# Layer 1 attention: probability blocks transposed by DVE and transfers, value products across the slot boundary, and four scalings for keys and queries

## The chip, the cores and the metric

The kernel runs on one core of one Trainium2 chip. The metric is the device time of one execution in microseconds, the median of several executions. The engines are TensorE (PE in the profile), VectorE (DVE), ScalarE (ACT), GpSimd (POOL) and SyncE (SP, which here only issues DMA transfers).

## The reference

Two transformer layers on 1024 tokens of width 512, in float32: layer 0 (linear attention with 32 heads, then experts), layer 1 (softmax attention with 32 heads of width 128, then a gated MLP with dequantised weights), each part followed by a residual and a layer norm. The change is in layer 1's attention:

```python
q = rmsnorm(hidden_states @ Wq + bq, gq)      # per head of 128
k = rmsnorm(hidden_states @ Wk + bk, gk)
v = hidden_states @ Wv + bv
scores = einsum('bnhd,bmhd->bhnm', q, k) / sqrt(128)
attn = softmax(scores, axis=-1)
out = einsum('bhnm,bmhd->bnhd', attn, v) @ Wo + bo
```

## The kernel before, in words

Every float32 matmul is made of three float32r matmuls (`three_pass`, lines 82 to 84): each operand is split into a high part (an ACT copy) and a low part (a subtraction on DVE or POOL), and high x high, high x low and low x high are added up in PSUM. So each tile that TensorE reads needs two more operations first.

`l1_attention` runs over 32 heads. Tokens are in 8 tiles of 128 (`NT`), and two tiles make a batch (`BATCH` = 2, four batches a head). Each engine has its own instruction queue, written out in order by a function `step` that is called once a head; it goes through 8 slots s = 0 to 7, and an engine that reaches a wait on a semaphore holds up everything behind it in its queue. Slots are software-pipelined: in slot s of head h an engine does

- the projection of one token tile of the next head (`project_tile` on TensorE, 12 matmuls of 384 columns; `take` on DVE adds the bias, L1434),
- in even slots the squares (`square`, ACT L1272), their sums and means (`means`, DVE L1441 and L1444), the inverse root on POOL (`inverse_rms`, L1236) and the scaling of the keys by it (`scale_k`, DVE L1449); in odd slots the transposes of keys and queries (`transpose_kq`, L1357), their high parts on ACT (L1279, L1280) and low parts on DVE (L1456, L1457); the query's own factor is put into the exponential,
- the scores of one query tile against all 1024 keys (`scores`, 6 matmuls of 512 columns into the banks `s_ps`), their row maximum and the shift made from it (`maxima`, DVE L1464 and L1466), and the exponential (`exponent`, ACT L1304, which writes `prob`),
- for the query tile of the slot before: 8 transposes of 128x128 on TensorE into `t_ps` (`transpose_probs`, L1390), the high part `pT_hi` (ACT L1298) and the low part `pT_lo` (DVE L1472),
- half of the value products of a finished batch (`values`, 12 matmuls of 256 columns into `o_ps`); behind the second half the parts of the output (ACT L1291, DVE L1484), and `output_tile` (3 matmuls of 512 columns) with the addition on DVE (L1493).

The heads 2 to 29 are a loop of two heads, the others are written out; the last head has no next head to project. The weights of a head come in one load (`AttentionWeights.load`) and are split in three pieces (L1039 on ACT, L1046 on POOL), the output weights in one (L1329, L1256). SP's queue issues three loads a head.

Layer 0 transposes its keys in another way (`move_k`, L352): DVE transposes blocks of 32x32 in place of the whole (L665), and 16 transfers move the 32-row groups to where they belong.

## Time and profile before

| what | value |
|---|---|
| median of 3 runs | 3258.07 us (3256.71 to 3260.59) |
| the profiled execution | 3259.28 us, its span 3257.5 us |
| busy share of the span: PE, DVE, ACT, POOL | 97%, 63%, 43%, 30% |
| mean granted TensorE clock | 0.991 of full speed |
| layer 1 attention | from about 1240 us to 2986 us |

The span is the time from the first to the last instruction. Busy time doesn't count waiting. A timeline row is one instruction (or a run of like ones, "x4"): start, length, engine, line, operation, tile written and tiles read; in brackets the idle time ahead of it and who ended it.

### The profile page before, as it was taken

How to read it: one execution, taken by the hardware profiler on the slowest of the kernel's cores; microseconds unless marked ns; L12 is line 12 of the kernel's file. 1: busy time of each engine (PE TensorE's matmuls, PEld its weight loads, DVE VectorE, ACT ScalarE, POOL GpSimd, SP SyncE). 2: the span in 40 equal slices, each digit the busy share in tenths (PEclk: the TensorE clock that was granted, in tenths of full speed). 3: DMA queues.
4: the chain of work that ended last, by engine and by line, in shares of the span. 5: the costliest groups of instructions: out<-in, count | busy, mean ns of one | idle time of the engine just before them, and what ended most of it. 6: DMA issues, size and time to landing. Idle time of an engine off the chain costs nothing. (4 is left out here: it accounts for less than half of the span.)

```text
span 3257.5 us, 58748 instructions
## 1 busy us (share of the span) xinstructions
PE 3165.4 (97%) x19680; PEld 2888.2 (89%) x19680; DVE 2067.9 (63%) x3445; ACT 1388.4 (43%) x2375; POOL 972.3 (30%) x819
## 2 busy tenths in 40 slices
PE   7999999999999978999999999999999999997998
PEld 7989989989989857999999999999999999996786
DVE  3445444455454457777777777777777777776555
ACT  3333333333333323555555555555555555554221
POOL 3333333333333322222222222222222222211765
PEclk9999999999999989999999999999999999999999
DMA  4122122122122101000000000000000000002541
GB/s 128 50 61 60 48 61 60 48 61 60 48 61 60 35 23 34 32 16 31 15 31 15 31 15 31 16 30 24 22 30 16 31 15 31 15 7 79 160 140 55
DMA packets 127177, 145.32 MB, mean 45 GB/s; under 512 B 15488, under 2 KB 91280, under 8 KB 126992
## 3 DMA queue, kind: packets, MB, share of 16 engines
q1 hardware_dynamic: 126272, 143.77, 14.7%
q8 instruction: 35, 0.57, 0.1%
q10 hardware_dynamic: 816, 0.79, 0.1%
q14 instruction: 22, 0.18, 0.0%
q0 software_dynamic: 32, 0.02, 0.0%
HBM read 125.63 MB, written 2.10 MB: 39 GB/s over the span
## 5 line engine op out<-in xcount | busy, mean ns | idle before, releaser
L1304 ACT ACTIVATE b_prob<-b_s_ps,b_shift,b_rstd 128x1024 f32<-128x1024 f32 x252 | 304.2, 1207 | 580.9 <-DVE b_shift L1466 580.9
L1464 DVE TENSOR_REDUCE b_row_max<-b_s_ps 128x1 f32<-128x1024 f32 x252 | 307.2, 1219 | 78.5 <-PE b_s_ps L84 78.4
L82 PE MATMUL b_pj_kq<-b_w_hi,xT_hi 128*128 128x384 f32 x1008 | 341.5, 339 | 1.2 <-DVE b_nat L1434 1.2
L84 PE MATMUL b_pj_kq<-b_w_hi,xT_lo 128*128 128x384 f32 x1008 | 341.9, 339 | 0.0
L83 PE MATMUL b_pj_kq<-b_w_lo,xT_hi 128*128 128x384 f32 x1008 | 341.5, 339 | 0.0
L506 ACT ACTIVATE a_sig<-a_pj 128x512 f32<-128x512 f32 x192 | 114.8, 598 | 486.7 <-PE a_pj L84 486.7
L82 PE MATMUL a_pj<-b_w_hi,xT_hi 128*128 128x256 f32 x1024 | 295.5, 289 | 11.7 <-DVE xT_lo L647 11.1
L84 PE MATMUL a_pj<-b_w_hi,xT_lo 128*128 128x256 f32 x1024 | 289.9, 283 | 0.0
L83 PE MATMUL a_pj<-b_w_lo,xT_hi 128*128 128x256 f32 x1024 | 289.4, 283 | 0.0
L1236 POOL TENSOR_TENSOR b_rstd<-b_mean_sq,power 128x4 f32<-128x4 f32 x128 | 128.9, 1007 | 527.7 <-DVE b_mean_sq L1444 524.4
L1390 PE MATMUL b_t_ps<-ident,b_prob 128*128 128x128 f32 x2048 | 265.6, 273 | 4.8 <-ACT b_prob L1304 4.4
L1046 POOL TENSOR_TENSOR b_w_lo<-b_w_raw,b_w_hi 128x512 fp32r<-128x512 f32 x96 | 123.2, 1285 | 486.3 <-ACT b_w_hi L1039 455.6
L706 DVE TENSOR_TENSOR a_kv_nat<-a_pj,a_sig 128x512 f32<-128x512 f32 x128 | 88.5, 692 | 273.0 <-ACT a_sig L506 271.8
L711 DVE TENSOR_TENSOR a_acc<-a_acc,a_y_ps 128x512 f32<-128x512 f32 x252 | 170.4, 676 | 136.1 <-PE a_y_ps L84 136.1
L1390 PEld LDWEIGHTS b_t_ps<-ident,b_prob 128*128 128x128 f32 x2048 | 230.5, 141 | 6.8 <-ACT b_prob L1304 6.8
L401 POOL TENSOR_TENSOR b_w_lo<-b_w_raw,b_w_hi 128x512 fp32r<-128x512 f32 x96 | 124.5, 1297 | 331.5 <-ACT b_w_hi L457 324.6
L82 PE MATMUL b_s_ps<-b_k_hi,b_q_hi 128*128 128x512 f32 x504 | 219.1, 435 | 0.0
L82 PEld LDWEIGHTS a_pj<-b_w_hi,xT_hi 128*128 128x128 f32 x1024 | 194.5, 190 | 14.6 <-issue 11.9
L1456 DVE TENSOR_TENSOR b_k_lo<-b_pj_kq,b_k_hi 128x256 fp32r<-128x256 f32 x128 | 54.3, 425 | 230.2 <-ACT b_q_hi L1280 230.2
L82 PEld LDWEIGHTS b_pj_kq<-b_w_hi,xT_hi 128*128 128x128 f32 x1008 | 189.1, 188 | 12.6 <-issue 1.7
L83 PEld LDWEIGHTS b_pj_kq<-b_w_lo,xT_hi 128*128 128x128 f32 x1008 | 189.2, 188 | 11.4
L84 PE MATMUL b_s_ps<-b_k_hi,b_q_lo 128*128 128x512 f32 x504 | 198.8, 394 | 0.0
(272 smaller groups left out, 9107.6 us busy)
## 6 DMA issues: line engine op xcount, KB each, us to landing
b_w_raw<-in_w SPq DMA_DIRECT2D x32, 768.0 KB, 4.3
b_w_raw<-in_w SPq DMA_DIRECT2D x95, 256.0 KB, 3.2
a_k_raw<-a_k_blocks SPq DMA_DIRECT2D x512, 32.0 KB, 1.8
a_w_raw<-in_w SPq DMA_DIRECT2D x32, 256.0 KB, 2.7
a_ow_raw<-in_ow SPq DMA_DIRECT2D x32, 256.0 KB, 3.1
...
```

The source lines that it names most:

```text
L82: pe.matmul(out, w_hi, x_hi, start=first, stop=False)
L83: pe.matmul(out, w_hi, x_lo, start=False, stop=False)
L84: return pe.matmul(out, w_lo, x_hi, start=False, stop=last)
L401: pool.tensor_tensor(w_lo[t][:, :, :], w_raw[t][:, :, :], f(w_hi[t][:, :, :]), ALU.subtract).then_inc(w_lo_done, 1)
L506: act.activation(out, pj[half][:, :], ACT.Sigmoid).then_inc(sig, 1)
L706: dve.tensor_tensor(out, pj[half][:, :], sig_tmp[half][:, :], ALU.mult).then_inc(silu, 1)
L711: dve.tensor_tensor(acc[:, t, :], acc[:, t, :], y_bank(h, t)[:, :], ALU.add).then_inc(y_added, 1)
L1046: pool.tensor_tensor(self.lo[b][:, :, cut], self.raw[:, :, cut], f(self.hi[b][:, :, cut]), ALU.subtract).then_inc(self.lo_done, 1)
L1236: pool.tensor_tensor(rstd[bg][:, BATCH * i:BATCH * (i + 1), :].rearrange("p t k -> p (t k)"), mean_sq[:, :, :].rearrange("p t k -> p (t k) ...
L1304: act.activation(prob[:, :], score_banks(h, t)[:, :], ACT.Exp, bias=shift[:, t:t + 1], scale=rstd[b][:, t, 1:2], accum_out=row_sum[:, t:t ...
L1390: last = pe.transpose(t_ps[:, cut], prob[:, cut], sh.ident[:, :])
L1464: dve.tensor_reduce(row_max[:, t:t + 1], score_banks(h, t)[:, :], AX_X, ALU.max).then_inc(max_done, 1)
```

## The change

The probabilities are no longer transposed by TensorE. DVE transposes 32x32 blocks of `prob` into `blocks` (`transpose_blocks`), for two query tiles; SP then issues 16 transfers (`move`) that carry 32-row groups into `pT_lo`, as raw values. ACT copies them to `pT_hi` in two halves of a batch (`prob_hi`), and POOL makes the low part in place (`prob_lo`), which was DVE's work. The value products and outputs of a batch come two slots later than before; the first half of a batch's value products stands at the end of an odd slot, the second half at the start of the even slot that follows. `s_ps` has two banks (the transposes' bank is free), `prob` two buffers. The row maximum is written negated as the shift. Keys and queries are both scaled by their inverse root, with four operations by a per-partition scalar for a batch (`scale_kq`), and the exponential has no scale. The weight splits stand in slots 1, 2 and 4 in place of 0, 2 and 4.

```diff
+        BLK = 32
+        GROUPS = P // BLK
+        MOVED = 16 * GROUPS * GROUPS
...
-        prob = sb("prob", [P, TOK])
-        row_max = sb("row_max", [P, NT])
+        prob = [sb(f"prob{i}", [P, TOK]) for i in range(2)]
+        blocks = [sb(f"blocks{i}", [P, GROUPS, NT, BATCH, BLK]) for i in range(2)]
...
-        pT_hi = [mlp.pT0[0], sb("pT_hi1", [P, NT, WIDE], F32R)]
-        pT_lo = [mlp.pT0[1], sb("pT_lo1", [P, NT, WIDE], F32R)]
+        pT_hi = [mlp.pT0[0], sb("pT_hi1", [P, GROUPS, NT, BATCH * BLK], F32R)]
+        pT_lo = [mlp.pT0[1], sb("pT_lo1", [P, GROUPS, NT, BATCH * BLK], F32R)]
...
-        s_ps = bank("s_ps", [P, TOK])
-        t_ps = bank("t_ps", [P, TOK])
+        s_ps = [bank(f"s_ps{i}", [P, TOK]) for i in range(2)]
...
-            n = (s - 3) % 8
-            if s >= 3:
+            n = (s - 5) % 8
+            if s >= 5:
...
+        def split_part(h, cur, rest, s):
+
+            n = (s - 4) % 8
+            if s >= 4:
+                return (h, n // 2, n % 2) if cur else None
+            return (h - 1, n // 2, n % 2) if rest else None
...
-            if s >= 5:
-                return (h, b, s - 5) if cur else None
-            return (h - 1, 1 - b, s + 3) if rest else None
+            if s >= 7:
+                return (h, b, s - 7) if cur else None
+            return (h - 1, 1 - b, s + 1) if rest else None
...
+        SPLITS = {1: 0, 2: 1, 4: 2}
...
+            def move(h, i):
+
+                sp.wait_ge(blocked, NT * h + BATCH * (i + 1))
+                to = f(pT_lo[i % 2][:, :, :, :])
+                for a in range(GROUPS):
+                    for g in range(GROUPS):
+                        sp.dma_start(to[a * BLK:(a + 1) * BLK, g].rearrange("p m n -> p (m n)"),
+                                     blocks[i % 2][g * BLK:(g + 1) * BLK, a].rearrange("p m u q -> p (m u q)")).then_inc(
+                            moved[i % 2], 16)
...
+            def step(h, b, cur, rest, nxt, more):
+                if cur and more:
+                    aw.load(sp, w, h + 2)
+                    load_bias(h + 2, b)
+                if rest:
+                    move(h - 1, NB - 1)
+                if cur:
+                    move(h, 0)
+                if nxt:
+                    load_output_weights(h + 1)
+                if cur:
+                    move(h, 1)
+                    move(h, 2)
...
+            def prob_lo(h, i, part):
+
+                pool.wait_ge(pT_hi_done, 2 * NB * h + 2 * i + part + 1)
+                cut = slice(part * NT // 2, (part + 1) * NT // 2)
+                pool.tensor_tensor(pT_lo[i % 2][:, :, cut, :], f(pT_lo[i % 2][:, :, cut, :]), f(pT_hi[i % 2][:, :, cut, :]),
+                                   ALU.subtract).then_inc(pT_lo_done, 1)
...
+            def prob_hi(h, i, part):
+
+                act.wait_ge(moved[i % 2], MOVED * (2 * h + i // 2 + 1))
                 wait(act, pv, NB * h + i - 1)
...
+                cut = slice(part * NT // 2, (part + 1) * NT // 2)
+                act.activation(pT_hi[i % 2][:, :, cut, :], f(pT_lo[i % 2][:, :, cut, :]), ACT.Copy).then_inc(pT_hi_done, 1)
 
             def exponent(h, b, t):
                 act.wait_ge(shift_done, NT * h + t + 1)
-                wait(act, p_tr, NT * h + t)
-                act.activation(prob[:, :], score_banks(h, t)[:, :], ACT.Exp, bias=shift[:, t:t + 1],
-                               scale=rstd[b][:, t, 1:2], accum_out=row_sum[:, t:t + 1]).then_inc(exp_done, 1)
+                wait(act, blocked, NT * h + t - 1)
+                act.activation(prob[t % 2][:, :], s_ps[t % 2][:, :], ACT.Exp, bias=shift[:, t:t + 1],
+                               accum_out=row_sum[:, t:t + 1]).then_inc(exp_done, 1)
...
+                pe.wait_ge(pT_lo_done, 2 * NB * h + 2 * i + part + 1)
                 if part == 0:
-                    pe.wait_ge(pT_lo_done, NT * h + BATCH * (i + 1))
...
+                    if s % 2 == 0 and quarter(h, b, cur, rest, s):
+                        values(*quarter(h, b, cur, rest, s))
...
-                    if quarter(h, b, cur, rest, s):
-                        values(*quarter(h, b, cur, rest, s))
                     if nxt and s % 2:
                         transpose_kq(h + 1, s // 2)
-                    if rest and s == 0:
-                        transpose_probs(h - 1, NT - 1)
-                    if cur and s:
-                        transpose_probs(h, s - 1)
...
+                    if s % 2 and quarter(h, b, cur, rest, s):
+                        values(*quarter(h, b, cur, rest, s))
...
-            def scale_k(g, bg, i):
+            def scale_kq(g, bg, i):
                 dve.wait_ge(rstd_ready, NB * g + i + 1)
-                dve.tensor_tensor(nat[i][:, :, 0:HD], nat[i][:, :, 0:HD],
-                                  rstd[bg][:, BATCH * i:BATCH * (i + 1), 0:1].broadcast_to([P, BATCH, HD]),
-                                  ALU.mult).then_inc(k_scaled, 1)
+                for u in range(BATCH):
+                    for k in range(2):
+                        part = nat[i][:, u, k * HD:(k + 1) * HD]
+                        last = dve.tensor_scalar(part, part, rstd[bg][:, BATCH * i + u, k:k + 1], None, ALU.mult)
+                last.then_inc(kq_scaled, 1)
...
-                dve.tensor_reduce(row_max[:, t:t + 1], score_banks(h, t)[:, :], AX_X, ALU.max).then_inc(max_done, 1)
-                dve.wait_ge(max_done, NT * h + t + 1)
-                dve.tensor_scalar(shift[:, t:t + 1], row_max[:, t:t + 1], rstd[b][:, t, 1:2], -1.0,
-                                  ALU.mult, ALU.mult).then_inc(shift_done, 1)
-
-            def prob_lo(h, t):
-                i, at = t // BATCH, (t % BATCH) * P
-                dve.wait_ge(pT_hi_done, NT * h + t + 1)
-                dve.tensor_tensor(pT_lo[i % 2][:, :, at:at + P], t_ps[:, :].rearrange("p (m n) -> p m n", m=NT),
-                                  f(pT_hi[i % 2][:, :, at:at + P]), ALU.subtract).then_inc(pT_lo_done, 1)
+                dve.tensor_reduce(shift[:, t:t + 1], s_ps[t % 2][:, :], AX_X, ALU.max, negate=True).then_inc(shift_done, 1)
...
+            def transpose_blocks(h, t):
+
+                i, u = t // BATCH, t % BATCH
+                dve.wait_ge(exp_done, NT * h + t + 1)
+                if u == 0:
+                    wait(dve, moved[i % 2], MOVED * (2 * h + i // 2))
+                dve.transpose(blocks[i % 2][:, :, :, u, :].rearrange("p a m q -> p m a q"),
+                              prob[t % 2][:, :].rearrange("p (m a q) -> p m a q", a=GROUPS, q=BLK)).then_inc(blocked, 1)
...
-                        prob_lo(h - 1, NT - 1)
+                        transpose_blocks(h - 1, NT - 1)
                     if cur and s:
-                        prob_lo(h, s - 1)
-                    if not early:
-                        for t in scored_in(h, cur, s):
-                            maxima(h, b, t)
+                        transpose_blocks(h, s - 1)
+                    for t in scored_in(h, cur, s):
```

DVE, an even slot in the loop (names as in the text above: `b_nat` are the projections, `b_o_lo` the output's low part). Before:

```order
L1441 TENSOR_REDUCE b_sq_sum<-b_sq 128x4
L1444 TENSOR_SCALAR b_mean_sq<-b_sq_sum 128x4
...
L1434 TENSOR_TENSOR b_nat<-b_pj_kq,b_bias 128x384
L1449 TENSOR_TENSOR b_nat<-b_nat,b_rstd 128x2x128
L1484 TENSOR_TENSOR b_o_lo<-b_o_ps,b_o_hi 128x256
L1472 TENSOR_TENSOR pT_lo<-b_t_ps,pT_hi 128x8x128
L1464 TENSOR_REDUCE b_row_max<-b_s_ps 128x1
L1466 TENSOR_SCALAR b_shift<-b_row_max,b_rstd 128x1
L1493 SCALAR_TENSOR_TENSOR x_nat<-b_y_ps,b_row_inv,x_nat 128x512
```

and with the change:

```order
L1468 TENSOR_REDUCE b_sq_sum<-b_sq 128x4
L1471 TENSOR_SCALAR b_mean_sq<-b_sq_sum 128x4
...
L1461 TENSOR_TENSOR b_nat<-b_pj_kq,b_bias 128x384
L1479 TENSOR_SCALAR b_nat<-b_nat,b_rstd 128x128 x4
L1513 TENSOR_TENSOR b_o_lo<-b_o_ps,b_o_hi 128x4x2x32
L1501 STREAM_TRANSPOSE b_blocks<-b_prob 128x8x4x32
L1493 TENSOR_REDUCE b_shift<-b_s_ps 128x1
L1522 SCALAR_TENSOR_TENSOR x_nat<-b_y_ps,b_row_inv,x_nat 128x512
```

The subtraction L1472 and the shift L1466 are gone, the block transpose L1501 stands ahead of the maximum L1493 in every slot, and the one scaling L1449 is four (L1479).

TensorE, an even slot, each block by its first rows (`b_pj_kq` is the projection, `b_o_ps` the value products, `b_s_ps` the scores, `b_y_ps` the output). Before:

```order
L82 MATMUL b_pj_kq<-b_w_hi,xT_hi 128x384
...
L84 MATMUL b_pj_kq<-b_w_hi,xT_lo 128x384
...
L82 MATMUL b_o_ps<-pT_hi,b_v_hi 128x256
...
L84 MATMUL b_o_ps<-pT_hi,b_v_lo 128x256
...
L1390 MATMUL b_t_ps<-ident,b_prob 128x128 x8
L82 MATMUL b_s_ps<-b_k_hi,b_q_hi 128x512
...
L82 MATMUL b_y_ps<-b_ow_hi,b_o_hi 128x512
```

and with the change:

```order
L82 MATMUL b_o_ps<-b_pT_hi,b_v_hi 128x256
...
L84 MATMUL b_o_ps<-b_pT_hi,b_v_lo 128x256
L82 MATMUL b_pj_kq<-b_w_hi,xT_hi 128x384
...
L84 MATMUL b_pj_kq<-b_w_hi,xT_lo 128x384
...
L82 MATMUL b_s_ps<-b_k_hi,b_q_hi 128x512
...
L82 MATMUL b_y_ps<-b_ow_hi,b_o_hi 128x512
```

The transposes L1390 are gone, and the value products stand ahead of the projection.

POOL, from an even slot to the next but one (`b_rstd` is the inverse root, `b_v_lo` the low part of the values, `b_w_lo` that of the weights). Before:

```order
L1236 TENSOR_TENSOR b_rstd<-b_mean_sq,power 128x4
L1243 TENSOR_TENSOR b_v_lo<-b_nat,b_v_hi 128x256
...
L1236 TENSOR_TENSOR b_rstd<-b_mean_sq,power 128x4
...
L1046 TENSOR_TENSOR b_w_lo<-b_w_raw,b_w_hi 128x4x128
L1243 TENSOR_TENSOR b_v_lo<-b_nat,b_v_hi 128x256
```

and with the change:

```order
L1267 TENSOR_TENSOR b_rstd<-b_mean_sq,power 128x4
...
L1281 TENSOR_TENSOR b_pT_lo<-b_pT_lo,b_pT_hi 128x4x256
L1274 TENSOR_TENSOR b_v_lo<-b_nat,b_v_hi 128x256
...
L1281 TENSOR_TENSOR b_pT_lo<-b_pT_lo,b_pT_hi 128x4x256
...
L1267 TENSOR_TENSOR b_rstd<-b_mean_sq,power 128x4
```

Behind each inverse root there is now a subtraction of 128x1024 for the probabilities (L1281), and another in the odd slot behind the values' low part.

## Rows read from the trace of the kernel before

**Rows 1.** Busy time by stretch (us, instructions), clock, DMA; layer 1 attention.
```profile
1600.00:2000.00 400.00, 400.00 (x2565) 377.01 (x2565) 297.16 (x506) 212.08 (x359) 89.62 (x90) 1.00 0.07 22
```

**Rows 2.** Timeline of ACT: start us, length us, line, operation, tiles.
```profile
1913.07 0.38 ACT L1279 ACTIVATE b_k_hi<-b_pj_kq 128x256 fp32r<-128x256 f32 x1 [0.75 <-PE b_pj_kq L1357]
1913.35 0.47 ACT L1280 ACTIVATE b_q_hi<-b_pj_kq,b_gain 128x256 fp32r<-128x256 f32 x1
1913.94 1.03 ACT L1298 ACTIVATE b_pT_hi<-b_t_ps 128x1024 fp32r<-128x1024 f32 x1
...
1924.20 1.21 ACT L1304 ACTIVATE b_prob<-b_s_ps,b_shift,b_rstd 128x1024 f32<-128x1024 f32 x1 [2.67 <-DVE b_shift L1466]
...
1925.40 0.62 ACT L1039 ACTIVATE b_w_hi<-b_w_raw 128x512 fp32r<-128x512 f32 x1
...
1977.84 1.21 ACT L1304 ACTIVATE b_prob<-b_s_ps,b_shift,b_rstd 128x1024 f32<-128x1024 f32 x1 [2.67 <-DVE b_shift L1466]
```

**Rows 3.** Timeline of TensorE (PE), first matmul of each block.
```profile
1986.51 1.04 PE L1390 MATMUL b_t_ps<-ident,b_prob 128*128 128x128 f32 x8
1987.30 0.47 PE L82 MATMUL b_s_ps<-b_k_hi,b_q_hi 128*128 128x512 f32 x1
...
1989.46 0.33 PE L82 MATMUL b_pj_kq<-b_w_hi,xT_hi 128*128 128x384 f32 x1
...
1991.57 0.28 PE L82 MATMUL b_o_ps<-pT_hi,b_v_hi 128*128 128x256 f32 x1
...
1992.99 0.60 PE L1357 MATMUL b_pj_kq<-ident,b_nat 128*128 128x128 f32 x4
```

**Rows 4.** Timeline of DVE, layer 0.
```profile
619.99 1.23 DVE L665 STREAM_TRANSPOSE a_k_blocks<-a_kv_nat 128x1024 f32<-128x1024 f32 x1
```

**Rows 5.** Timeline of DVE, layer 1.
```profile
1959.67 0.17 DVE L1444 TENSOR_SCALAR b_mean_sq<-b_sq_sum 128x4 f32<-128x4 f32 x1
...
1961.31 0.42 DVE L1484 TENSOR_TENSOR b_o_lo<-b_o_ps,b_o_hi 128x256 fp32r<-128x256 f32 x1
...
1962.93 1.21 DVE L1464 TENSOR_REDUCE b_row_max<-b_s_ps 128x1 f32<-128x1024 f32 x1
...
1964.96 0.55 DVE L1434 TENSOR_TENSOR b_nat<-b_pj_kq,b_bias 128x384 f32<-128x384 f32 x1
1965.43 0.15 DVE L1480 RECIPROCAL b_row_inv<-b_row_sum 128x2 f32<-128x2 f32 x1
```

**Rows 6.** Timelines of DVE and POOL at the layer norms and the first head.
```profile
1237.81 1.91 DVE L169 TENSOR_SCALAR x_nat<-x_nat,ln_mv,ln_rstd 128x512 f32<-128x512 f32 x4
...
1256.74 1.48 DVE L1449 TENSOR_TENSOR b_nat<-b_nat,b_rstd 128x256 f32<-128x256 f32 x1
...
1256.67 1.26 POOL L1046 TENSOR_TENSOR b_w_lo<-b_w_raw,b_w_hi 128x512 fp32r<-128x512 f32 x1
...
2999.68 0.89 DVE L169 TENSOR_SCALAR x_nat<-x_nat,ln_mv,ln_rstd 128x512 f32<-128x512 f32 x1
```

**Rows 7.** Groups of POOL instructions, 1500 to 2700 us: busy us, mean ns.
```profile
L1046 POOL TENSOR_TENSOR b_w_lo<-b_w_raw,b_w_hi 128x512 fp32r<-128x512 f32 x67 | 85.7, 1280 | 358.6 <-ACT b_w_hi L1039 358.6
L1243 POOL TENSOR_TENSOR b_v_lo<-b_nat,b_v_hi 128x256 fp32r<-128x256 f32 x89 | 66.2, 743 | 113.9 <-ACT b_v_hi L1285 113.9
```

**Rows 8.** Timelines of SP and ACT, layer 0: sixteen transfers and their reader.
```profile
32.07 10.12 SPq L352 DMA_DIRECT2D a_k_raw<-a_k_blocks  x16
...
43.45 0.63 ACT L474 ACTIVATE a_k_T<-a_k_raw 128x512 f32<-128x512 f32 x1 [5.83 <-DMA a_k_raw<-a_k_blocks]
```

**Rows 9.** Timeline of TensorE: a value product after a wait.
```profile
2951.74 0.39 PE L82 MATMUL b_o_ps<-pT_hi,b_v_hi 128*128 128x256 f32 x1 [0.30 <-DVE pT_lo L1472]
```

**Rows 10.** Timelines of ACT and DVE, the last head.
```profile
2942.54 1.21 ACT L1304 ACTIVATE b_prob<-b_s_ps,b_shift,b_rstd 128x1024 f32<-128x1024 f32 x1 [2.67 <-DVE b_shift L1466]
...
2973.91 1.20 ACT L1304 ACTIVATE b_prob<-b_pj_kq,b_shift,b_rstd 128x1024 f32<-128x1024 f32 x1
...
2985.47 0.75 DVE L1493 SCALAR_TENSOR_TENSOR x_nat<-b_pj_kq,b_row_inv,x_nat 128x512 f32<-128x512 f32 x1
```

More of the change, by code:

```diff
@@ L1117, in l1_attention @@
         y_ps = bank("y_ps", [P, HALF])
-        ln_banks = [s_ps[:, 0:HALF], s_ps[:, HALF:], t_ps[:, 0:HALF], t_ps[:, HALF:]]
+        ln_banks = [s[:, j * HALF:(j + 1) * HALF] for s in s_ps for j in range(2)]
         w_lo_done, proj = aw.lo_done, aw.proj
@@ L1257, in step @@
                                            ALU.subtract).then_inc(ow_lo_done, 1)
-                    if nxt and more and s in (0, 2, 4):
-                        aw.split_low(pool, h + 2, b, s // 2)
+                    if nxt and more and s in SPLITS:
+                        aw.split_low(pool, h + 2, b, SPLITS[s])
             steps(pool, step)
@@ L1375, in scores @@
                     pe.wait_ge(kq_lo_done, NB * (h + 1))
-                wait(pe, exp_done, NT * h + (t - 1 if peeled(h, HEADS - 1) and t else t))
+                wait(pe, exp_done, NT * h + t - 1)
                 cut = slice(t * P, (t + 1) * P)
@@ L1380, in scores @@
                     keys = slice(j * HALF, (j + 1) * HALF)
-                    last = three_pass(pe, score_banks(h, t)[:, keys], q_hi[b][:, cut], q_lo[b][:, cut],
+                    last = three_pass(pe, s_ps[t % 2][:, keys], q_hi[b][:, cut], q_lo[b][:, cut],
                                       k_hi[b][:, keys], k_lo[b][:, keys], True, True)
                 last.then_inc(scored, 1)
-            def transpose_probs(h, t):
-                pe.wait_ge(exp_done, NT * h + t + 1)
-                wait(pe, pT_lo_done, NT * h + t)
-                for m in range(NT):
-                    cut = slice(m * P, (m + 1) * P)
-                    last = pe.transpose(t_ps[:, cut], prob[:, cut], sh.ident[:, :])
-                last.then_inc(p_tr, 1)
             def output_tile(h, b, t):
```

66 lines of the change are left out of this document (27 added, 39 removed).

## The prediction

> **What bounds the kernel now.** I read the table of busy time by stretch first. In a stretch of 400 us inside layer 1's attention TensorE is busy for 400.00 us at full clock, DVE for 297, ACT for 212, POOL for 90 [rows 1]. So this stage goes by the sum of its matmuls, and the view of waits agrees: it names no wait of TensorE there, only of the other engines. Then the timelines. The reader should see that DVE and ACT hand work to each other in every slot, and that this has cover only because a slot is long. On ACT the same slot's exponentials lie 53.64 us apart from one head to the next (1924.20 to 1977.84) [rows 2]: four pairs of an even and an odd slot, 13.41 us a pair.
>
> **What is removed.** TensorE loses eight transposes a slot: they start at 1986.51 and the scores at 1987.30, 0.79 us [rows 3], 6.3 us a head. If TensorE stayed the bound, a head would take 47.4 us. The question is whether the rest of the loop can run in 11.8 us a pair.
>
> **What is added, by engine.** DVE: the subtraction of 128x1024 leaves and a block transpose of the same size comes, 1.23 us in layer 0 [rows 4]; the shift leaves; one scaling a pair becomes four of 128x128. A DVE operation that waits for nothing starts 0.08 us before the end of the one ahead (0.55 long, the next after 0.47) [rows 5]. Four scalings of 128x512 by per-partition scalars take 1.91 us, so 0.46 apart [rows 6]; one operation of 128x4 lasts 0.17 [rows 5], so 0.09 apart. By columns 128x128 comes to 0.18; I take 0.20, 0.80 for four, bounds 0.36 and 1.84. POOL: two subtractions of 128x1024 a pair. The rows give 0.743 for 256 columns and 1.280 for 512 [rows 7], 2.1 ns a column, so 2.37; upper bound twice 1.28, 2.56. SP: 16 transfers a pair, each of 32 rows of 2 KB. Layer 0 issues such 16 with rows of 1 KB in 10.12 us from 32.07 on, and ACT reads them at 43.45, 11.38 us after the first issue [rows 8]. That is 10.1 of 13.4 us a pair, and three loads a head beside it, so SP isn't the bound if an issue doesn't grow with its row. ACT's amount of work stays.
>
> **The chain that I expect to set the pace.** It is closed through all four engines, from the row maximum of an even slot to that of the next even slot. A hand-over costs some 0.05. (1) Maximum 1.21 + 0.05 [rows 5]. (2) Exponential, 1.20 to ACT's next start (1924.20 to 1925.40) [rows 2]. (3) In the odd slot the copies of values, keys and queries, all ahead of the probability copy in ACT's queue: 0.28 for the keys, the same for the values, 0.37 for the queries (ACT starts 0.10 before the end of the one ahead), 0.93 [rows 2]. (4) Probability copy, second half: 1.03 + 0.05 [rows 2]. (5) POOL's subtraction of that half: 2.37 + 0.05. (6) TensorE: the second half of the value products stands first in the even slot and waits for it: 12 matmuls, 1.42 [rows 3], and 0.11 for the start after a wait (0.39 beside 0.28) [rows 3, 9]. (7) Behind it the projection, 2.11 [rows 3], and an estimated 0.20 until its last result can be read. (8) DVE takes the projection, 0.47 [rows 5]. (9) Four scalings, 0.80. (10) Low part of the output, 0.34 [rows 5]. (11) Block transpose, 1.15, then the maximum. Sum: 1.26 + 1.20 + 0.93 + 1.08 + 2.42 + 1.53 + 2.31 + 0.47 + 0.80 + 0.34 + 1.15 = 13.49 us a pair. In slots 2 and 4 a weight copy stands between (2) and (3), 0.62 long, 0.52 to the next [rows 2]. A head: 4 x 13.49 + 1.04 = 55.0 us, 1.3 above the 53.7 of now. So what TensorE saves turns into waiting, some 8 us a head, ahead of the second value half.
>
> Before the change no such chain passed through TensorE and POOL together: POOL did nothing for the probabilities, and the value products came behind the projection.
>
> **Edges.** 29 heads of this kind: +38. Head 0 has no values before slot 5 and head 30 projects nothing in slots 6 and 7. Both are some 2 us shorter than the others now, since TensorE has less to do in them, and less of the new chain falls away there than of TensorE's sum; I add an estimated 2 and 3. Head 31 has no projections, and its seven steps from exponential to exponential take 31.4 us (2942.54 to 2973.91) [rows 10]. After, a batch's transfers are in a chain of two pairs: 11.5 + 1.08 + 4.79 (two halves on POOL) + 1.7 + 0.8 + 1.23 = 21.1, 10.5 a pair, 36.6 for seven steps: +5. The drain, from the last exponential to the end of the last addition (2985.47 + 0.75), is 12.3 us [rows 10]. After: exponential 1.2, transpose 1.28, transfers 11.5, 1.08, 4.79, values 1.7, output copies 0.9, two outputs 1.6, addition 0.75 = 24.8: +12.5. Together 38 + 5 + 5 + 12.5 = 61. The profiled execution took 3259.28 us with a span of 3257.5, 1.2 above the median of 3258.07, so the same difference holds for both: 3258 + 61 = **3319 us**, 1.9% slower.
>
> **What is hidden, and by what.** Transfers: a batch is blocked 0.08 us after the maximum of an even slot starts and has landed 11.5 later. The odd slot's maximum comes 5.4 after the even one (1.26 + 1.20, copies 0.56, low keys and queries an estimated 1.24, transpose 1.15), so counted from it the batch lands at 6.2. Its first copy on ACT ends at 7.2; behind it waits the exponential of the even slot, due only at 5.8 + 0.80 + 0.34 + 1.15 + 1.26 = 9.3. So the transfers have two us of cover, and each further one goes into the chain. The second bank of the scores and the factor that leaves the exponential (now applied in the scaling of queries) cost nothing: no score waits.
>
> **A rule against this change.** The row first: before the loop the scaling of the keys (two SBUF inputs) took 1.48 us at 1256.74, while POOL subtracted from 1256.67 on for 1.26, where 256 columns take 0.42 elsewhere [rows 5, 6]; and a 128x512 scaling by per-partition scalars took 0.89 at 2999.68, where four take 1.91 otherwise [rows 6], with a subtraction on POOL in both cases. In the loop the scalings come right behind POOL's inverse root, and POOL's next work is a first-half subtraction. By my times the scalings run from 5.8 (1.45 for POOL's half, + 1.53 + 2.31 + 0.47) to 6.6 us after the odd maximum, and the subtraction starts at 7.2, after slots with a weight copy at 6.7. They miss each other, by 0.6 us in two pairs of a head and 0.1 in the other two; at these times the rows add nothing.
> The Trainium skill, SBUF — State Buffer, section "Who interferes with whom", says that a `tensor_scalar` in a two-port mode and a GpSimd operation exclude each other, and that the one that came first holds the ports to its end. The trace agrees with it (1.48 for 0.42). By it the sum would be 2.4 higher in every pair in which POOL comes first.
>
> **Rivals.**
> A, POOL and the scalings meet (slower still). If transfers land 0.3 us earlier or the scalings take 0.3 longer, then in two pairs a head the last scaling waits for POOL's 2.37: +4.7 a head, 29 x 4.7 = 136, 3455 us; in all four pairs, from some 0.8 on, 3530 or more. Against: a row of 2 KB lands later than one of 1 KB, if anything.
> B, transfers are the bound: if an issue goes with its bytes, 16 x 1.27 = 20 us a pair, a head 83, some 4100 us. Against: from the end of the last issue to the reader's start there are 1.3 us (43.45 - 42.19) [rows 8], so the bytes of a transfer don't hold the queue for long.
> C, the other sign: POOL's half is ready earlier than I have it, and the chain doesn't pass through TensorE. Then a pair goes by DVE and ACT alone, over squares, means and POOL's root, which I estimate to be ready at 5.1 where the take ends at 5.8: 12.8 us; with scalings at 0.36, 12.4, and four weight copies of 0.52: a head 51.7, 29 x -2.0 - 5 + 17 = -46, 3212 us. It decides at a pair of 13.0 us: below that the kernel is faster. With TensorE the bound after all it would be 3258 - 29 x 6.3 - 10 + 17 = 3082. For it: DVE would be busy for some 40 of 47 us only. Against: nearly each term of the 13.49 is a row.
> D, nothing measurable: the chain is 0.5 shorter, and heads gain what the edges lose.
>
> **How the numbers follow.** Forecast 0.45, its own range from the scalings (0.36; or 1.2) and POOL's 2.56, 116 pairs: -51 and +70, so 3268 to 3390. A 0.25, B 0.05, C 0.14, D 0.05; others of the same sign as the forecast (a slower copy out of SBUF, a clock that falls in the gap of the drain) 0.06. The range 3240 to 3470 leaves out B, most of C and the worst of A. Faster by over 0.2% 0.14, within 0.2% (about what three runs can tell here) 0.05, slower 0.81.
>
> **What would show it.** In the loop TensorE busy for some 47 of 55 us, waiting at the first value matmul of even slots for POOL's low parts; DVE's take waiting for the projection; POOL's subtractions 2.4 us long; SP issuing 64 transfers in 40 of 55 us; scalings of 0.28 us. Wrong if scalings last 1 us and more (A), if ACT's copies wait for transfers and exponentials behind them (B), if TensorE is busy throughout or the scalings wait for the root alone (C).

## The result

The changed kernel takes 3526.8 us (median of four executions, 3484.56 to 3529.72) where the kernel before takes 3257.8 (3256.71 to 3260.59): 1.080 times, 95% interval 1.073 to 1.087. The profiled execution is the fastest of the four, 3484.56 us with a span of 3482.8, and what is read below is its trace. The forecast was 3319 us, slower, with a range up to 3470: the direction was right, the size was not.

Busy time by stretch after the change (columns as in [rows 1]): TensorE (first busy column) 336 us of 400 instead of 400, POOL (last) 201 instead of 90, and the granted clock, 1.00 before, is 0.95.

```profile
1600.00:2000.00 400.00, 336.19 (x1847) 305.59 (x1846) 273.81 (x476) 176.35 (x314) 201.14 (x130) 0.95 0.36 90
```

The page's groups of the new operations, for [rows 2, 5 and 7]: busy us, mean ns, idle before. Each operation has nearly the length that was forecast for it. What stands out is the idle time.

```profile
L1343 ACT ACTIVATE b_prob<-b_s_ps,b_shift 128x1024 f32<-128x1024 f32 x256 | 285.5, 1115 | 722.0 <-DVE b_shift L1493 722.0
L1281 POOL TENSOR_TENSOR b_pT_lo<-b_pT_lo,b_pT_hi 128x1024 fp32r<-128x1024 f32 x128 | 303.5, 2371 | 166.8 <-ACT b_pT_hi L1338 166.8
L1501 DVE STREAM_TRANSPOSE b_blocks<-b_prob 128x1024 f32<-128x1024 f32 x256 | 316.1, 1235 | 4.5 <-ACT b_prob L1343 4.5
L1493 DVE TENSOR_REDUCE b_shift<-b_s_ps 128x1 f32<-128x1024 f32 x256 | 303.7, 1186 | 2.0 <-PE b_s_ps L84 2.0
L1461 DVE TENSOR_TENSOR b_nat<-b_pj_kq,b_bias 128x384 f32<-128x384 f32 x252 | 139.1, 552 | 241.7 <-PE b_pj_kq L84 241.6
```

From one head's first exponential to the next the trace shows 53.7, 55.1, 55.3, 58.2 us, and from the ninth such step on 61.4 or 61.5 (but for the last two). The forecast had 55.0 for all. So a head as forecast exists, at the start of the stage, and then something is added. It is added by the pair: of the 119 pairs of slots in heads 1 to 30, 69 take 13.4 to 14.1 us from odd maximum to odd maximum and 50 take 16.6 to 17.3. The slow ones are always the same two of a head, the pair around slot 4 and the pair around slot 6. Here is one pair of each kind. First DVE in the quick one: maximum at 2041.09, take of the projection at 2046.44 (5.35 later; forecast 5.3), four scalings 0.86 long, next odd maximum at 2054.55, 13.46 later (forecast 13.49).

```profile
2041.09 1.18 DVE L1493 TENSOR_REDUCE b_shift<-b_s_ps 128x1 f32<-128x1024 f32 x1
...
2046.44 0.56 DVE L1461 TENSOR_TENSOR b_nat<-b_pj_kq,b_bias 128x384 f32<-128x384 f32 x1 [1.48 <-PE b_pj_kq L84]
2046.91 0.86 DVE L1479 TENSOR_SCALAR b_nat<-b_nat,b_rstd 128x128 f32<-128x128 f32 x4
...
2054.55 1.19 DVE L1493 TENSOR_REDUCE b_shift<-b_s_ps 128x1 f32<-128x1024 f32 x1
```

POOL's first-half subtraction in that pair starts 0.71 us after the scalings have ended (the forecast said 0.6):

```profile
2048.48 2.40 POOL L1281 TENSOR_TENSOR pT_lo<-pT_lo,pT_hi 128x1024 fp32r<-128x1024 f32 x1 [2.44 <-ACT pT_hi L1338]
```

Then the slow one, DVE and POOL. The take is 7.11 us after the maximum, the four scalings last 2.46 us, and they lie inside POOL's subtraction (2014.18 to 2016.58). The next odd maximum is 17.26 later.

```profile
2007.21 1.19 DVE L1493 TENSOR_REDUCE b_shift<-b_s_ps 128x1 f32<-128x1024 f32 x1
...
2014.32 0.56 DVE L1461 TENSOR_TENSOR b_nat<-b_pj_kq,b_bias 128x384 f32<-128x384 f32 x1 [2.72 <-PE b_pj_kq L84]
2014.79 2.46 DVE L1479 TENSOR_SCALAR b_nat<-b_nat,b_rstd 128x128 f32<-128x128 f32 x4
2017.17 0.41 DVE L1513 TENSOR_TENSOR b_o_lo<-b_o_ps,b_o_hi 128x256 fp32r<-128x256 f32 x1
...
2022.58 0.42 DVE L1485 TENSOR_TENSOR b_k_lo<-b_pj_kq,b_k_hi 128x256 fp32r<-128x256 f32 x1 [1.54 <-ACT b_q_hi L1320]
...
2024.47 1.19 DVE L1493 TENSOR_REDUCE b_shift<-b_s_ps 128x1 f32<-128x1024 f32 x1
2014.18 2.40 POOL L1281 TENSOR_TENSOR pT_lo<-pT_lo,pT_hi 128x1024 fp32r<-128x1024 f32 x1 [1.49 <-ACT pT_hi L1338]
```

Why is the take late? TensorE in the two pairs, first matmul of the value half, of the projection, and of the scores behind it. In the slow pair:

```profile
2008.78 0.39 PE L82 MATMUL b_o_ps<-b_pT_hi,b_v_hi 128*128 128x256 f32 x1 [2.16 <-POOL b_pT_lo L1281]
...
2010.46 0.52 PE L82 MATMUL b_pj_kq<-b_w_hi,xT_hi 128*128 128x384 f32 x1
...
2013.96 0.39 PE L82 MATMUL b_s_ps<-b_k_hi,b_q_hi 128*128 128x512 f32 x1
```

and in the quick one:

```profile
2042.58 0.39 PE L82 MATMUL b_o_ps<-b_pT_hi,b_v_hi 128*128 128x256 f32 x1 [2.45 <-POOL b_pT_lo L1281]
...
2044.12 0.34 PE L82 MATMUL b_pj_kq<-b_w_hi,xT_hi 128*128 128x384 f32 x1
...
2046.24 0.39 PE L82 MATMUL b_s_ps<-b_k_hi,b_q_hi 128*128 128x512 f32 x1
```

Both begin 1.5 to 1.6 us after the maximum, behind a wait of 2.2 and 2.45 us. But the projection takes 3.50 us in one and 2.12 in the other. The same stretches by the microsecond (the third number from the end is the granted clock) show what differs: the clock is at its half level, 1.2 instead of 2.4 GHz.

```profile
2009.00:2010.00 1.00, 1.00 (x10) 1.00 (x10) 0.05 (x1) 1.00 (x3) 0.00 (x0) 1.00 0.55 131
2010.00:2011.00 1.00, 1.00 (x6) 1.00 (x6) 0.29 (x1) 0.90 (x3) 0.71 (x1) 0.56 0.37 88
2011.00:2012.00 1.00, 1.00 (x4) 1.00 (x4) 0.56 (x2) 0.16 (x1) 0.89 (x2) 0.50 0.46 109
2012.00:2013.00 1.00, 1.00 (x4) 1.00 (x4) 0.00 (x0) 0.00 (x0) 0.69 (x1) 0.50 0.49 94
2013.00:2014.00 1.00, 1.00 (x6) 1.00 (x6) 0.00 (x0) 0.96 (x1) 0.00 (x0) 0.74 0.70 223
2014.00:2015.00 1.00, 1.00 (x6) 0.83 (x5) 0.68 (x2) 0.10 (x1) 0.82 (x1) 1.00 0.03 10
```

So this slow pair takes 3.80 us more than the quick one. 1.38 of it is the projection and 0.38 the value half, the start and the take's own wait at the lower clock (scalings 7.58 instead of 5.82 us after the maximum); 1.60 is the length of the scalings; the last 0.44 is not new, it is a weight copy on ACT that this pair has and the other hasn't (DVE's wait for the queries' copy 1.54 instead of 1.10), and was in the forecast. Compared with a quick pair of the same place in the head, a slow one costs 3.2 us around slot 4 (17.25 beside 14.0) and 3.1 around slot 6 (16.63 beside 13.55): the scalings start 1.6 later and last 1.5 to 1.8 longer. Over heads 1 to 30 the granted clock stands at half in 51 spells, 178 us in all, and in none in the kernel before; each of the 50 slow pairs has one, and no quick pair has. The slow pairs come to 157 us (23 x 3.2 + 27 x 3.1). Added to the forecast that gives 3476, and with the 8 us by which the drain was too short (below) 3484, beside 3484.56 measured; the closeness is partly luck, since the quick heads (55.1 to 55.3) and the edges were a little off too. This is a reading of one trace; it doesn't show which of the two causes the other, nor whether either would cost anything alone. The theory (M): the clock falls after TensorE's wait for POOL, that makes the take late, and the late scalings meet POOL. The rivals: POOL and the scalings meet whatever the clock (L); the clock has no part in it (N); the landing of the transfers sets the pace and the rest only fills it (T); the form of the four scalings is dear by itself (F).

### The profile page after: what moved, and what is told of

Read it like the earlier page. It is cut to its first block and busy times, and to the rows that moved or that the text cites. A ratio compares the mean times of both kernels' runs of the same rounds, so it can differ in the third digit from the quotient of the medians.

```text
span 3482.8 us, 57425 instructions
## 1 busy us (share of the span) xinstructions
PE 3079.6 (88%) x17632; PEld 2755.3 (79%) x17632; DVE 2113.5 (61%) x3573; ACT 1344.6 (39%) x2375; POOL 1578.8 (45%) x1075
## 5 line engine op out<-in xcount | busy, mean ns | idle before, releaser
L1343 ACT ACTIVATE b_prob<-b_s_ps,b_shift 128x1024 f32<-128x1024 f32 x256 | 285.5, 1115 | 722.0 <-DVE b_shift L1493 722.0
L82 PE MATMUL b_pj_kq<-b_w_hi,xT_hi 128*128 128x384 f32 x1008 | 376.3, 373 | 7.7 <-DVE b_nat L1461 7.7
L1281 POOL TENSOR_TENSOR b_pT_lo<-b_pT_lo,b_pT_hi 128x1024 fp32r<-128x1024 f32 x128 | 303.5, 2371 | 166.8 <-ACT b_pT_hi L1338 166.8
L1281 POOL TENSOR_TENSOR pT_lo<-pT_lo,pT_hi 128x1024 fp32r<-128x1024 f32 x128 | 304.1, 2376 | 165.0 <-ACT pT_hi L1338 165.0
L1501 DVE STREAM_TRANSPOSE b_blocks<-b_prob 128x1024 f32<-128x1024 f32 x256 | 316.1, 1235 | 4.5 <-ACT b_prob L1343 4.5
L1493 DVE TENSOR_REDUCE b_shift<-b_s_ps 128x1 f32<-128x1024 f32 x256 | 303.7, 1186 | 2.0 <-PE b_s_ps L84 2.0
L1461 DVE TENSOR_TENSOR b_nat<-b_pj_kq,b_bias 128x384 f32<-128x384 f32 x252 | 139.1, 552 | 241.7 <-PE b_pj_kq L84 241.6
L82 PE MATMUL b_o_ps<-b_pT_hi,b_v_hi 128*128 128x256 f32 x512 | 154.2, 301 | 143.8 <-POOL b_pT_lo L1281 143.8
L82 PE MATMUL b_o_ps<-pT_hi,b_v_hi 128*128 128x256 f32 x512 | 152.3, 297 | 134.8 <-POOL pT_lo L1281 134.8
L82 PEld LDWEIGHTS b_o_ps<-b_pT_hi,b_v_hi 128*128 128x128 f32 x512 | 99.7, 195 | 160.5 <-POOL b_pT_lo L1281 157.7
```

The costliest lines, as they stand in the source:

```text
L82: pe.matmul(out, w_hi, x_hi, start=first, stop=False)
L1281: pool.tensor_tensor(pT_lo[i % 2][:, :, cut, :], f(pT_lo[i % 2][:, :, cut, :]), f(pT_hi[i % 2][:, :, cut, :]), ALU.subtract).then_inc(pT_l ...
L1343: act.activation(prob[t % 2][:, :], s_ps[t % 2][:, :], ACT.Exp, bias=shift[:, t:t + 1], accum_out=row_sum[:, t:t + 1]).then_inc(exp_done, 1)
L1461: dve.tensor_tensor(nat[i][:, u, :], project_bank(g, t), bias_sb[bg][:, :], ALU.add).then_inc(taken, 1)
L1493: dve.tensor_reduce(shift[:, t:t + 1], s_ps[t % 2][:, :], AX_X, ALU.max, negate=True).then_inc(shift_done, 1)
L1501: dve.transpose(blocks[i % 2][:, :, :, u, :].rearrange("p a m q -> p m a q"), prob[t % 2][:, :].rearrange("p (m a q) -> p m a q", a=GROUPS ...
```

## The experiments

**TensorE kept busy in its wait.** This tells the clock from the rest: nothing is taken away, work is added.

```
 if s % 2 == 0 and quarter(h, b, cur, rest, s):
+    (heads 1 to 30) wait(pe, kq_lo_done, NB * (h + 1) + s // 2)
+    for _ in range(20): pe.transpose(kq_ps[:, 0, 0:P], sh.ident[:, :], sh.ident[:, :])
     values(*quarter(h, b, cur, rest, s))
```

> Edit: TensorE gets 20 more 128x128 transposes of the identity (0.10 us each, 2.0 us) in every even slot of heads 1 to 30, ahead of its wait for POOL's low parts, into a bank that nobody reads then; their results are not used. It adds work and takes no wait away. Theory M (the clock is the cause of the late projection): the granted clock stays at 1.00 through the projection, the take comes 1.3 us earlier in the pairs that were late, and the scalings then end before POOL's subtraction starts: heads of 55 to 57 us instead of 61.4, the kernel 3330 to 3400. Rival L (POOL and the scalings meet whatever the clock): only the 1.3 us in two pairs of a head come back, 3450. Rival N (the clock has no part in it, or the transposes do not hold it): 3527 or more, since the added transposes can only delay.

Measured: 3349.7 us (1.028, 1.026 to 1.030). One spell at half clock over heads 1 to 30, no four scalings over 0.88 us, heads of 55.9. Some 177 us came back by giving TensorE 240 us more to do. Rivals L and N fall. But TensorE was now busy for 399.81 of 400 us: 47.4 us of its own and 8.0 of transposes a head, so the transposes themselves may have set this pace. Hence half of them (range(10)):

> Edit: the changed kernel with 10 transposes of the identity ahead of TensorE's wait instead of 20: 1.0 us a pair. With 20 the sum of TensorE's work was 47.4 + 8.0 = 55.4 of a head of 55.9 us, so that run may have been bound by the transposes themselves; with 10 the sum is 51.4. Theory M (the closed chain of 13.5 us sets the pace when the clock stays up, and half of the gap filled is enough to keep it up): heads of 54.5 to 55.5 us, no long scalings, 3310 to 3345. Rival (10 are too few: the clock falls as in the changed kernel): 3450 or more.

Measured: 3331.0 us (1.023, 1.021 to 1.024), heads of 55.2 and 55.4, no spell and no long scaling. TensorE's wait in it, ten transposes and then 0.46 us for POOL:

```profile
2005.76 1.25 PE L1436 MATMUL b_pj_kq<-ident 128*128 128x128 f32 x10
2007.46 0.38 PE L82 MATMUL b_o_ps<-pT_hi,b_v_hi 128*128 128x256 f32 x1 [0.46 <-POOL pT_lo L1281]
```

That is the kernel of the forecast, 0.4% above its 3319. In its pairs around slot 6 the last of the four scalings, begun before POOL, ends 0.1 us after POOL has started and is as short as ever (0.87 for the four).

**The scalings ahead of the take.** They don't depend on it, only on POOL's root.

```
 if nxt and s % 2 == 0: means(h + 1, s // 2)
+if nxt and s % 2 == 0: scale_kq(h + 1, 1 - b, s // 2)
 if projected(...): take(...)
 ...
-if nxt and s % 2 == 0: scale_kq(h + 1, 1 - b, s // 2)
```

> Edit: in even slots the four scalings come ahead of DVE's take of the projection, on which they do not depend; nothing else. Theory M (TensorE's clock stands at half for a spell after its wait for POOL's low parts, the projection and the take come some 1.3 us late in some pairs, and the scalings behind the take then fall into POOL's first-half subtraction, 2.4 us instead of 0.87): the scalings start when the root is ready, some 2.5 us ahead of POOL's subtraction, every four of them take 0.87, and the chain has no scalings in it any more. A pair goes by 13.5 - 0.8 = 12.7 us, with 1.3 more in the pairs whose projection is at half clock: a head 52 to 55 us instead of 61.4, the kernel 3260 to 3350. Rival T (the landing of the transfers and ACT's copies behind it set the pace; the scalings only fill a wait): 3500 to 3530, heads of 61 us.

Measured: 3316.4 us (1.018, 1.016 to 1.020), heads of 54.3 and 54.9. The four scalings take 0.87 or 0.88 us in every pair of the loop, and there are 13 spells at half clock over heads 1 to 30 instead of 51. So the collisions have a part in bringing the spells about, not only the other way. TensorE's longest wait in heads 1 to 30 is 2.2 us here, where the changed kernel has waits of 3.0. The spells that are left fall in the value half and the projection; a pair with one takes 14.6 us instead of 14.1 in the same place, 6.5 us for all 13.

**Both.** Scalings first, and 20 transposes.

> Edit: both single edits together: the scalings ahead of the take in even slots, and 20 transposes of the identity ahead of TensorE's wait. Neither the lock nor the clock is left. Theory M (each is a cost of its own): the chain is 13.5 - 0.8 us long at full clock, a head 55.9 - 3.2 = 52.7 us instead of the 54.6 with the scalings first alone, the kernel 3350 - 29 x 3.2 = 3257. Rival (with the scalings out of the chain the low clock costs nothing any more): 3316 or more, as with the scalings first alone, since the transposes are added work.

Measured: 3341.7 us (1.026, 1.024 to 1.028). The theory's 3257 is missed. The number lies where the rival put it (3316 or more), but it decides nothing, since neither had counted TensorE's sum: it is busy for 400 of 400 us, 55.5 a head as 47.4 + 8.0 says. With ten:

> Edit: the scalings ahead of the take, and 10 transposes of the identity ahead of TensorE's wait. With 20 of them TensorE was busy for 400 of 400 us (55.5 us a head, of which 8.0 the transposes), so that run could not show what the clock costs. Theory M (each is a cost of its own): 13.5 - 0.8 = 12.7 a pair at full clock, a head 52 to 53 us, 3240 to 3270, where the scalings first alone gave 54.6 and 3316. Rival (no cost of the low clock is left once the scalings are out of the way): 3310 to 3330.

Measured: 3313.1 us (1.017, 1.016 to 1.019), heads of 54.3 and 54.4, one spell. The rival was right here: once the scalings are out of POOL's way, the spells that are left cost 3 us by the medians and 6.5 by the two profiled executions (3316.40 and 3309.87), 0.5 a spell. And the pair is 13.6 us, not my 12.7. DVE now waits for POOL's root, not for TensorE, and the take stands in the same ring behind it:

```profile
2019.05 0.88 DVE L1483 TENSOR_SCALAR b_nat<-b_nat,b_rstd 128x128 f32<-128x128 f32 x4 [1.12 <-POOL b_rstd L1267]
2019.84 0.55 DVE L1465 TENSOR_TENSOR b_nat<-b_pj_kq,b_bias 128x384 f32<-128x384 f32 x1
```

**The lock at full clock.** The other half of the theory: with the clock held, push the scalings into POOL's subtraction by hand (six operations of 128x4 on DVE ahead of them, beside the 20 transposes).

```
 def scale_kq(g, bg, i):
+    for j in range(6): dve.tensor_scalar(junk[:, 4*j:4*j+4], bo_sb[:, 4*j:4*j+4], 1.0, None, ALU.mult)
     dve.wait_ge(rstd_ready, NB * g + i + 1)
```

> Edit: the kernel of the run before in which TensorE gets 20 transposes of the identity ahead of its wait (its heads take 55.9 us at full clock, its scalings end 0.2 to 0.5 us before POOL's first-half subtraction starts in two pairs of a head, and within 0.1 us of it in the other two), and in it six DVE operations of 128x4 (0.09 us each, some 0.5 in all) between the take and the scalings. Their results are not used. Theory L (a scaling and POOL's subtraction exclude each other, whatever the clock, and the prediction's threshold of 0.3 us was right): scalings of 2.3 to 2.6 us for four at full clock, in two pairs a head or in all four: heads of 55.9 + 2.0 + 2 or 4 x 1.7, 61.3 to 64.7 us, the kernel 3510 to 3610. Rival (the scalings were long in the changed kernel because of something that goes with the low clock): heads of 57.9 us, 3408.

Measured: 3472.6 us (1.066, 1.064 to 1.068), below the expected 3510 and far above the rival's 3408. Of the 119 sets of four scalings in heads 1 to 30, 41 are long, 3.0 us, and the clock doesn't fall once there; heads alternate between 61.3 and 59.0. One of the long ones, POOL in it, and the shortest, the median and the longest of its four operations in ns:

```profile
2020.52 0.52 DVE L1481 TENSOR_SCALAR b_junk<-b_bo_sb 128x4 f32<-128x4 f32 x6
2020.95 3.01 DVE L1486 TENSOR_SCALAR b_nat<-b_nat,b_rstd 128x128 f32<-128x128 f32 x4
2021.44 2.42 POOL L1282 TENSOR_TENSOR pT_lo<-pT_lo,pT_hi 128x1024 fp32r<-128x1024 f32 x1 [1.47 <-ACT pT_hi L1339]
L1486 DVE TENSOR_SCALAR b_nat<-b_nat,b_rstd x4: 280/282/2421, 2020.9 to 2021.5; 128x128 f32<-128x128 f32 x4
```

Three of the four scalings take 0.28 us. The last starts at 2021.5, behind POOL's start, takes 2.42 and ends (2023.96) with POOL (2023.86). POOL's own operation is hardly longer than elsewhere (2.42 beside 2.40). Six tiny operations, 0.43 us from first start to the scalings' start, cost 123 us. My sum took them all as delay; they moved the scalings by 0.3 to 0.45 in the pairs around slots 4 and 6 (from 6.0 or 6.1 to between 6.3 and 6.5 after the maximum) and by 0.1 in the others, and only pairs of the first kind met.
The Trainium skill, SBUF — State Buffer, section "Who interferes with whom", has it that the one that comes first holds the shared ports for its whole instruction and the other is blocked. The trace agrees for a series of operations as for one: POOL came in between two of the four, and the one behind it took 2.42 us instead of 0.28. (The prediction's row for the same rule, 1.48 for 0.42, was of an operation with two SBUF inputs; this one is a `tensor_scalar`.)

**One scaling instead of four.** The third part of the change undone: the keys alone in one multiplication, the queries' factor in exponential and shift.

```
-for u in range(BATCH): for k in range(2): dve.tensor_scalar(part, part, rstd[...], None, ALU.mult)
+dve.tensor_tensor(nat[i][:, :, 0:HD], nat[i][:, :, 0:HD], rstd[...].broadcast_to([P, BATCH, HD]), ALU.mult)
```

> Edit: the third part of the change alone is undone: one multiplication of the keys by a broadcast factor (128x2x128, two SBUF inputs) instead of four scalings by per-partition scalars, and the queries' factor in the exponential and in the shift again; transfers and the value products across the boundary stay. Theory M (what is lost is lost because DVE works on SBUF late, when POOL subtracts, whatever the form of the operation): the one multiplication starts as late as the first scaling did, behind POOL's start in two pairs a head, and takes 1.5 to 2.4 us there; the shift is an operation more in the chain: 3500 to 3570. Rival F (it is the form of the four operations that costs): heads of 54 to 56 us, 3330 to 3390.

Measured: 3349.0 us (1.028, 1.027 to 1.030). I missed, and the number is the rival's. The reason is not quite the rival's either: of 119 multiplications in heads 1 to 30, 9 are long (1.6 to 1.8 us instead of 0.41), each of them in a pair with a spell at half clock, and there are 11 spells. The form is not immune, it is shorter by 0.45 us, and a collision costs it 1.2 instead of 1.6. The nearest reading is that this keeps the loop out of the slow pattern; no run changes the length alone, so it isn't shown. That the four scalings are not dear by themselves, without POOL's subtractions, shows this run, in which they alone are put into the kernel before:

> Edit: the kernel before, and of the change the third part alone: four scalings by per-partition scalars for keys and queries, no factor in the exponential, the negated maximum in one operation. No transfers, TensorE transposes the probabilities as before. Both theories: TensorE is busy throughout and nothing waits for DVE longer than before, POOL subtracts nothing for the probabilities, so 3252 to 3265, no change. If the four scalings were dear by themselves: over 3265.

Measured: 3258.7 us (1.0002, 0.9992 to 1.0011; ten executions). No change.

**The projection ahead of the value half.** Only the wait's place differs, as before the change.

```
-if s % 2 == 0 and quarter(...): values(...)
 if projected(...): project_tile(...)
+if s % 2 == 0 and quarter(...): values(...)
```

> Edit: in even slots the second half of the value products stands behind the projection on TensorE, as before the change, so that the wait for POOL's low parts no longer holds the projection up; nothing else. Theory M: the take comes 2 to 4 us earlier, the scalings wait for the root alone and end ahead of POOL's subtraction (0.87 each four), and the chain through TensorE is shorter by the projection, the take and the scalings: 13.49 - 2.31 - 0.47 - 0.80 + 0.4 for the output's copy = 10.3, so the pair goes by DVE and ACT (12.4 to 12.8 us) or by TensorE (11.8): a head 47.5 to 52, the kernel 3090 to 3230. Rival T (transfers and ACT's copies set the pace): the wait only moves behind the projection, 3450 or more.

Measured: 3246.0 us (0.996, 0.995 to 0.998), heads of 52.5, one spell, all scalings 0.87 or 0.88: faster than the kernel before, and 16 us above the top of what I expected. T falls: transfers and copies are the same, and 281 us are gone.

**DVE's order on top of it.** In that kernel DVE waits for squares and for the queries' copy with a block transpose ready behind. First I moved it ahead in both slots:

```
 for s in range(NT):
+    (the block transposes of the slot, the one with u == 1 behind wait(dve, pv, NB * h + i - 1))
     if nxt and s % 2 == 0: means(h + 1, s // 2)
```

> Edit: the kernel with the projection first on TensorE in even slots, and in it DVE's block transpose as the first operation of each slot, in the gaps in which DVE waited for the squares (1.14 to 1.66 us) and for the copy of the queries (1.10 to 1.54 us); the second one of a batch also waits for the value products two batches earlier, so that the transfers don't overwrite what TensorE reads. Theory (with the wait out of the projection's way a pair goes by DVE and ACT, and only the order on DVE keeps it above TensorE's sum): some 0.9 us less in the even slot and 1.1 in the odd one, more than the 1.4 us that a pair stands above TensorE's 11.8: heads of 47.5 to 49 us instead of 52.5, the kernel 3090 to 3150. Rival T (the landing of the transfers and the copies behind it set the pace): heads stay at 52 us, 3230 to 3250.

Measured: 3512.3 us (1.077, 1.076 to 1.079). Fully wrong. The transfers start earlier by a transpose and more, so POOL's subtraction comes right behind its root, just as the scalings start:

```profile
2009.57 2.99 DVE L1479 TENSOR_SCALAR b_nat<-b_nat,b_rstd 128x128 f32<-128x128 f32 x4 [0.55 <-POOL b_rstd L1267]
2009.51 2.38 POOL L1281 TENSOR_TENSOR pT_lo<-pT_lo,pT_hi 128x1024 fp32r<-128x1024 f32 x1
```

This happens in every pair, and at the wait that I had to add DVE stands for 2.2 us a pair (260.5 us in 121 waits); the run doesn't tell the two costs apart. The clock stays up (two spells in 30 heads; no wait of TensorE in the loop is over 1.4 us), with TensorE busy for 335 of 400 us, about as in the changed kernel (336): collisions need no low clock. Moved in odd slots only (`if cur and s % 2`), without the added wait:

> Edit: the kernel with the projection first on TensorE in even slots (heads of 52.5 us), and in it the block transpose as DVE's first operation in odd slots only; in even slots it stays where it was, behind the scalings. The run with both moved showed every four scalings inside POOL's subtraction (2.98 us) and DVE waiting for the value products; neither comes from the odd slot. Theory (in the odd slot DVE waits 1.10 to 1.54 us for the copy of the queries while the exponential that the transpose needs is long done, so the transpose fits into the wait and the odd maximum comes some 1.0 us earlier; counted from it POOL's subtraction comes 1.0 later, further away from the scalings): a pair 13.1 - 1.0 = 12.1, near TensorE's 11.8: heads of 48 to 49.5 us, the kernel 3120 to 3175. Rival T (landing and copies set the pace): 3235 to 3250. Rival L (the earlier odd maximum brings the scalings into a subtraction again): over 3300.

Measured: 3170.4 us (0.9735, 0.9722 to 0.9748): 2.7% faster than the kernel before, 10% faster than the changed one, with every part of the change in it. Heads are 49.9 and 50.0, TensorE is busy for 386 of 400 us, scalings end mostly 1.2 to 2.0 us before POOL starts and never less than 0.7. In the odd slot DVE waits 0.71 us for the exponential and then does without a gap what it did around 1.1 to 1.5 us of waiting:

```profile
2008.18 1.25 DVE L1501 STREAM_TRANSPOSE b_blocks<-b_prob 128x1024 f32<-128x1024 f32 x1 [0.71 <-ACT b_prob L1343]
2009.35 0.52 DVE L1461 TENSOR_TENSOR b_nat<-b_pj_kq,b_bias 128x384 f32<-128x384 f32 x1
2009.79 0.14 DVE L1509 RECIPROCAL b_row_inv<-b_row_sum 128x2 f32<-128x2 f32 x1
2009.85 0.40 DVE L1485 TENSOR_TENSOR b_k_lo<-b_pj_kq,b_k_hi 128x256 fp32r<-128x256 f32 x1
```

**The changed kernel once more**, for a second profile.

> No edit: the changed kernel once more, for a second profile. The profiled execution was the fastest of four (3484.56 us beside a median of 3526.8), so its trace may hold fewer slow pairs than usual. In that trace a pair with a half-clock spell over the projection and scalings inside POOL's subtraction takes 3.35 us more than one without. Theory M: a slower execution has more such pairs, 12 or 13 for 42 us, and nothing else is different in it: uncollided scalings still 0.87, moves and copies as before. Rival: something else differs (transfers land later, all pairs a little longer).

Measured: median 3503.1 us of five, 3482.75 to 3515.08 (1.075, 1.073 to 1.077). The profiled one was again the fastest, with the same number of slow pairs, 50 of 119, so no trace shows a slower execution. What there is of the others: spans of 3481.0, 3491.2, 3501.3, 3502.0 and 3513.3 us go with mean clocks of 0.962, 0.960, 0.958, 0.957 and 0.957. A fall from 0.962 to 0.957 is (0.043 x 3513.3 - 0.038 x 3481.0) x 2 = 38 us more at half clock, for 32 us of time. That fits more slow pairs; it doesn't show them.

## Why the forecast was right in kind and wrong in size

**Right.** The closed chain through four engines is there. Its pair without a spell is 13.46 us beside the forecast's 13.49, POOL's subtraction 2.37 (2.37), block transpose 1.235 (1.15 + 0.08), exponential 1.12 (1.20), the four scalings 0.79 from start to the next start (0.80), take 5.35 us after the maximum (5.3), POOL 7.4, and 7.0 around slot 4 (7.2, 6.7). TensorE waits 1.4 to 3.1 us ahead of the second value half, and DVE's take waits for the projection. With the clock held up the kernel takes 3331 where the forecast says 3319. In the last head seven steps take 36.67 us (3142.43 to 3179.10; forecast 36.6, though its 21.1 for two pairs comes to 36.9).

**The step that failed** is "They miss each other, by 0.6 us in two pairs of a head and 0.1 in the other two; at these times the rows add nothing." The gaps themselves were near: 0.6 us and more in nearly all quick pairs around slots 0 and 6, 0.45 to 0.65 in most around slot 2 and 0.03 to 0.25 in most around slot 4 (forecast 0.1 for both). What failed is that they rested on (6) and (7) at full clock: "12 matmuls, 1.42 [rows 3]" and "Behind it the projection, 2.11 [rows 3]", read from a kernel in which TensorE never waits. The forecast itself makes TensorE wait some 2 us in every pair, and thought of a falling clock only in the drain. In 50 of 119 pairs the projection ran at half clock and took some 3.5 us, the scalings came 1.6 us later than in the same place without a spell, and a margin of 0.1 or 0.6 was gone. Rival A had the collisions, with another trigger (earlier transfers or longer scalings) and without the lateness: "+4.7 a head", where two slow pairs add 6.2 (61.4 beside 55.2), about half of it the scalings' length and half their lateness. It was given 0.25, and the range up to 3470 took in its lower branch without the slow clock.

**The loss feeds itself.** With the clock held, collisions vanish (3527 to 3331 us, no spell left). With the collisions taken away by order, or the scaling made 0.45 us shorter, the spells fall from 51 to 13 and 11. Neither edit touches the other cause. The trace of the changed kernel shows one link. By its length, TensorE's wait ahead of the second value half comes in four groups in heads 1 to 30: 1.4 to 1.7 us (33 pairs, no spell), 2.0 to 2.2 (36 pairs, 27 with a spell), 2.4 to 2.5 (27, none) and 3.0 to 3.1 (23, all with a spell). The 23 longest are those around slot 6 behind a slow pair around slot 4. Where the pair around slot 4 was quick, the wait around slot 6 was at most 2.2, and 4 of 6 such pairs were slow. So one slow pair makes the next wait longer, and the next pair is then always slow. It ends there: the pair around slot 0 waits 2.4 to 2.5 and never has a spell. In the order with the scalings first, 13 spells without a collision behind them cost 3 to 6.5 us (3316 beside 3313, or by the profiled executions). The lock alone, at full clock, costs 123 us with a push of 0.45 us or less (3473 beside 3350).

**The drain** was forecast to be 24.8 us and is 32.8 (3179.10 to 3211.86). 5.3 of the missing 8 are an omitted wait: the block transpose of the last tile stands behind the low part of an output in DVE's queue, and that waits for the value products of the batch ahead, which themselves run at half clock (granted 0.50 from 3179.64 to 3184.20). The transfers land 1.2 us later after the transpose than forecast (12.7 beside 11.5), and the last value half, again at half clock (0.50 from 3203.05 to 3208.20), takes 1.2 longer.

```profile
3185.26 0.42 DVE L1513 TENSOR_TENSOR b_o_lo<-b_o_ps,b_o_hi 128x256 fp32r<-128x256 f32 x1 [5.10 <-ACT b_o_hi L1331]
3185.60 1.23 DVE L1501 STREAM_TRANSPOSE b_blocks<-b_prob 128x1024 f32<-128x1024 f32 x1
```

**What stays open.** Why the clock falls in one pair and not in another: a wait of 2.0 to 2.2 us has a spell behind it in 27 of 36 pairs, one of 2.4 to 2.5 in none of 27, and with the scalings first 13 of 45 waits of 2.1 to 2.2 us have one. So the length of the wait alone doesn't tell, and nor does it tell why the pair around slot 4 is slow again in head after head. Why executions of the changed kernel differ by 45 us where those of the others agree within 11.
